# A transformer layer on one core: projections in two pieces, semaphores by part, later coefficient loads, an inverse root on GpSimd, and the third hidden tile first

## The reference

```
x = layernorm(x + attn(x))        # x: 4 batches x 512 tokens x 512
x = layernorm(x + ffn(x))
attn: q,k,v = x @ Wq.T, x @ Wk.T, x @ Wv.T   # 32 query heads of 16, 8 key/value heads (4 queries share one)
      q,k = rope(q), rope(k)
      out = softmax(causal(q k.T / 4)) v ;  out @ Wo.T
ffn:  W = mean_w + mean(|w - mean_w|) * sign(w - mean_w)     # for w1, w2, w3 (512 x 1792)
      silu(x @ W1.T) * (x @ W3.T) @ W2.T
layernorm: (x - mean) / sqrt(var + 1e-5)
```

## Time and profile before

| | us |
|---|---|
| median of 3 runs (lowest, highest) | 992.41 (990.38, 994.47) |
| profiled execution, device time | 995.51 |
| its span from first to last instruction | 993.7 |
| PE busy, PEld busy | 897.1, 609.5 |
| DVE busy | 719.9 |
| ACT busy | 354.0 |
| POOL busy | 258.2 |

### The profile page before, as it was taken

How to read it: one execution, slowest core, us unless ns; L and a number is a source line. 1 busy time by engine, 2 the same in 40 slices (tenths; PEclk the granted TensorE clock), 3 DMA queues, 4 the chain that set the end, 5 groups by cost and what they waited for, 6 DMA issues and landing times.

```text
span 993.7 us, 15538 instructions
## 1 busy us (share of the span) xinstructions
PE 897.1 (90%) x5186; PEld 609.5 (61%) x5186; DVE 719.9 (72%) x1896; ACT 354.0 (36%) x681; POOL 258.2 (26%) x323
## 2 busy tenths in 40 slices
PE   3278998899998999899897999999999999999993
PEld 2144444355443545444476888888888888888882
DVE  7587775776776777766558778777877787778777
ACT  0126665655765556654932111111111111111133
POOL 2046444654357342411333010111011101110000
PEclk9579999999999999999998999999999999999997
DMA  5747776745567623420341011011101110110004
GB/s 174 93 152 175 217 193 209 175 152 137 124 183 189 149 73 82 104 67 23 131 161 63 1 64 42 23 63 63 60 3 63 63 63 0 63 63 0 1 12 159
DMA packets 49692, 95.28 MB, mean 96 GB/s; under 512 B 11424, under 2 KB 25760, under 8 KB 48608
## 3 DMA queue, kind: packets, MB, share of 16 engines
q1 hardware_dynamic: 49632, 94.53, 34.1%
HBM read 66.72 MB, written 14.02 MB: 81 GB/s over the span
## 4 chain that ended last, share of the span: by engine, by line
PE 73%; DVE 11%; DMA 6%; issue 4%; SPq 3%; ACT 2%; POOL 1%; ACTq 0%; DVEq 0%; POOLq 0%
PE PS L970 19%; PE PS L971 18%; PE PS L972 18%; PE PS L1069 5%; PE PS L1096 5%; DVE masked L822 5%; PE PS L1086 4%; DMA Qs<-parts 2%; PE PS L1088 2%; SPq L352 1%; DMA xraw<-xt 1%; DMA o_dram<-Oe 1%; DVE rp L814 1%; ACT Pt L612 1%; DMA Qs<-wo 1%
## 5 line engine op out<-in xcount | busy, mean ns | idle before, releaser
L822 DVE CUSTOM_DVE_ANT_0 masked<-PS,mkw 128x384 bf16<-128x384 f32 (+3 forms) x512 | 230.3, 485 | 109.8 <-PE PS L1069 107.1
L612 ACT ACTIVATE Pt<-PS 128x512 f32<-128x512 f32 (+1 forms) x352 | 190.6, 562 | 153.7 <-PE PS L1088 132.8
L1069 PE MATMUL PS<-Ks,Qs 96*128 96x384 bf16 (+3 forms) x512 | 134.0, 314 | 46.9 <-DVE negM L822 31.2
L970 PE MATMUL PS<-XH,WH 128*128 128x512 f32 x448 | 174.4, 389 | 0.7 <-DVE XL L777 0.7
L972 PE MATMUL PS<-XH,WL 128*128 128x512 f32 x448 | 174.3, 389 | 0.0
L971 PE MATMUL PS<-XL,WH 128*128 128x512 f32 x448 | 174.3, 389 | 0.0
L565 ACT ACTIVATE sg<-PS 128x512 f32<-128x512 f32 x56 | 33.6, 600 | 371.1 <-PE PS L972 371.1
L1086 PE MATMUL PS<-Qs,Ks 99*128 99x256 bf16 (+3 forms) x512 | 139.8, 306 | 3.8 <-DMA Qs<-mT 1.9
L724 DVE TENSOR_TENSOR y<-PS,y 128x512 f32<-128x512 f32 x224 | 138.9, 681 | 1.1 <-PE PS L972 1.1
L472 POOL TENSOR_TENSOR Wr<-Wr 128x512 f32<-128x512 f32 x42 | 53.8, 1312 | 312.6 <-DMA Wr<-wall 312.6
L1069 PEld LDWEIGHTS PS<-Ks,Qs 96*128 96x128 bf16 x512 | 41.4, 99 | 149.5 <-DVE negM L822 100.7
(11 more groups left out here) (101 smaller groups left out, 1233.6 us busy)
## 6 DMA issues: line engine op xcount, KB each, us to landing
co<-wall SPq DMA_DIRECT2D x42, 512.0 KB, 5.7
Wr<-wall SPq DMA_DIRECT2D x42, 512.0 KB, 4.8
Qs<-parts SPq DMA_DIRECT2D x96, 128.0 KB, 3.9
o_dram<-Oe SPq DMA_DIRECT2D x32, 256.0 KB, 3.4
xraw<-xt SPq DMA_DIRECT2D x16, 256.0 KB, 4.0
Oc<-o_dram SPq DMA_DIRECT2D x16, 256.0 KB
y<-x SPq DMA_DIRECT2D x4, 1024.0 KB, 8.2
Inv<-inv_dram SPq DMA_DIRECT2D x16, 256.0 KB
```

The source lines that it names most:

```text
L612: act.activation(Pt[:, t % 2, h:h + m, P * t:S], PS[:, BANKS_P2[(g[0] * NU + n) % 3], 0:m * w].rearrange("p (m w) -> p m w", m=m), ACT.Exp ...
L822: least = dve.tensor_tensor_reduce(masked[:, (g[0] * NU + n) % 2, i * w:(i + 1) * w], bank, mkw[:, S - w:S], -1.0, -MASKED, ALU.add, ALU.m ...
L970: pe.matmul(dst, stH, moH, start=(k == 0), stop=False)
L1069: last = pe.matmul(bank[:, i * w:(i + 1) * w], Qs[0:ROWS, GH * g[1] + h0 + i, P * t:P * (t + 1)], Ks[0:ROWS, g[1], 0:w], start=True, stop= ...
```

## The change

- `project` runs in two pieces of six products, at units 4 and 7, instead of four pieces of three at 3, 5, 7 and 8. `project_out` runs in two pieces of six, at units 8 and 10 (in step 7: 1 and 3), instead of 3, 3 and 6. The two first-pass banks are the same before and after.
- `q_in` and `k_kept` count by part (high, middle, low) instead of by tile. So `high` waits only for the high parts of the tile before, `middle` for the middle ones, and `low` (POOL) for the low one. PE waits for the same transfers as before, through three semaphores.
- The two loads `co` leave the head of SP's list for a step. The first stands behind the maxima `mT` and ahead of the stacking, the second behind the stacking. `diff` and `abs_sum` come one step later, and the first `abs_sum` at unit 5 instead of 8.
- POOL computes the inverse root as a power of -0.5; DVE's reciprocal and ACT's Sqrt go.
- In `first_pair`, DVE makes the third hidden tile (`silu(2, 0)`) ahead of the first `accumulate`, and the third weight tile after the second `accumulate`.

```diff
-PROJECT_AT = (3, 5, 7, 8)
+PROJECT_AT = (4, 7)
...
+BEFORE = {1: (1, 0), 2: (2, 0), 4: (3, 0), 5: (0, 1), 6: (K_TILE, 1)}
...
-        q_in = [sem(f"q_in{i}") for i in range(4)]
-        k_kept = sem("k_kept")
+        q_in = [sem(f"q_in{p}") for p in range(3)]
+        k_kept = [sem(f"k_kept{p}") for p in range(3)]
...
+            def stacked(eng, b, tile, part):
+                eng.wait_ge(q_in[part], 16 * Q_PARTS.count(part) * (QT * b + tile + 1))
+
+            def sent(eng, ps, b, part):
+                tile, late = BEFORE[ps]
+                if tile == K_TILE:
+                    eng.wait_ge(k_kept[part], 16 * (b + late))
+                else:
+                    stacked(eng, b + late, tile, part)
...
-                                             parts[:, part, :]).then_inc(q_in[i], 16)
+                                             parts[:, part, :]).then_inc(q_in[part], 16)
...
-                            if sec.nxt and st < NCO // 2:
-                                load_co(b, 2 * st)
-                                load_co(b, 2 * st + 1)
...
                                 sp.dma_start(Qs[ROWS:ROWS + 3, h:h + GH, :], mT[:]).then_inc(max_in, 16)
+                            if sec.nxt and st < NCO // 2:
+                                load_co(b, 2 * st)
...
                                 stacks(tile, b + (who == "nxt"), r + b * N_ROPE, 2)
+                            if sec.nxt and st < NCO // 2:
+                                load_co(b, 2 * st + 1)
...
-                            if sec.nxt and st < NCO // 2:
-                                diff(b, 2 * st)
+                            if sec.nxt and 0 < st <= NCO // 2:
+                                diff(b, 2 * st - 2)
...
+                                sent(pool, ps, b, 2)
                                 low(r)
-                            if sec.nxt and st < NCO // 2:
-                                diff(b, 2 * st + 1)
+                            if sec.nxt and 0 < st <= NCO // 2:
+                                diff(b, 2 * st - 1)
...
+                            pool.wait_ge(var_out, b)
+                            pool.tensor_tensor(rs[:], sd[:], expo[:], ALU.pow).then_inc(std_out, 1)
                             pool.wait_ge(std_out, b)
                             pool.tensor_tensor(shift[:], mean[:], rs[:], ALU.mult).then_inc(shift_out, 1)
...
-                        act.wait_ge(var2_out, b + 1)
-                        act.activation(rs[:], sd[:], ACT.Sqrt).then_inc(std2_out, 1)
                         act.wait_ge(shift2_out, b + 1)
...
-                                    before = {1: (1, b + 1), 2: (2, b + 1), 4: (3, b + 1), 5: (0, b + 2),
-                                              6: (K_TILE, b + 2)}[ps]
-                                    if before[0] == K_TILE:
-                                        act.wait_ge(k_kept, before[1] * 48 - 48)
-                                    else:
-                                        act.wait_ge(q_in[before[0]], before[1] * 96)
+                                    sent(act, ps, b, 0)
                                     high(r)
                                 if n == 4 and sec.behind(st, 3):
                                     o_copy(sec.behind(st, 3))
                                 if n == 7 and mine:
+                                    sent(act, ps, b, 1)
                                     middle(r)
-                                if n in (8, 10) and sec.nxt and st < NCO // 2:
-                                    abs_sum(b, 2 * st + (n == 10))
-                                if n == 7 and st == 7 and sec.prev:
-                                    act.wait_ge(var_out, b)
-                                    act.activation(rs[:], sd[:], ACT.Sqrt).then_inc(std_out, 1)
+                                if n in (5, 10) and sec.nxt and 0 < st <= NCO // 2:
+                                    abs_sum(b, 2 * st - 2 + (n == 10))
...
                         if n == 2:
-                            act.wait_ge(q_in[0], 96)
+                            stacked(act, 0, 0, 0)
                         high(r)
+                        if n == 2:
+                            stacked(act, 0, 0, 1)
                         middle(r)
                     sections(Run(act, section))
...
-                        a = flink(dve.tensor_scalar(sd[:], mv[:, :, 1], EPS, None, ALU.add))
-                        dve.wait_ge(fchain, a)
-                        dve.reciprocal(sd[:], sd[:]).then_inc(var2_out, 1)
+                        dve.tensor_scalar(sd[:], mv[:, :, 1], EPS, None, ALU.add).then_inc(var2_out, 1)
...
+                            if first and u == 0:
+                                dve.wait_ge(y_done, QT)
+                                silu(2, 0)
                             if first and u == 2:
                                 for m in range((B - 1) * KT + 2, B * KT):
                                     turned_low(m)
-                            if not (last and u == UNITS - 1) and not (first and u == 0):
+                            if not (last and u == UNITS - 1) and not (first and u < 2):
...
                             if first and u == 0:
-                                weights(3, 1, 2)
+                                pass
                             elif b < 3 and not (last and i == 1) and not (first and i == 0):
                                 weights(it * 6 + 3 * i + 3, (i + 1) % 2, b)
                             accumulate(n, FIRST_PAIR[u] % B if first else b)
+                            if first and u == 1:
+                                weights(3, 1, 2)
                             if last and i == 1:
...
                         dve.wait_ge(mid_out, r + 1)
+                        if n == 2:
+                            stacked(dve, 0, 0, 2)
                         dve.tensor_tensor(parts[:, 2], rp[:, 1], parts[:, 1], ALU.subtract).then_inc(lo_out, 1)
...
-                                    pe.wait_ge(q_in[st // 2], (b + 1) * 96)
+                                    for p in range(3):
+                                        stacked(pe, b, st // 2, p)
...
-                                    project(b + (who == "nxt"), tile, up, PROJECT_AT.index(n))
+                                    for k in range(2 * PROJECT_AT.index(n), 2 * PROJECT_AT.index(n) + 2):
+                                        project(b + (who == "nxt"), tile, up, k)
...
-                                    for k in ({1: (0,), 2: (1,), 3: (2, 3)} if st == 7 else {7: (0,), 9: (1,), 10: (2, 3)}
+                                    for k in ({1: (0, 1), 3: (2, 3)} if st == 7 else {8: (0, 1), 10: (2, 3)}
                                               ).get(n, ()):
```

More of the change, by code:

```diff
@@ L236, in layer @@
         asum = top.enter_context(nc.sbuf_tensor("asum", [P, 3, NCO], F32))
-        few = top.enter_context(nc.sbuf_tensor("few", [P, 6, QT], F32))
-        csum, coef, sd, mean, shift, rs = (few[:, n] for n in range(6))
+        few = top.enter_context(nc.sbuf_tensor("few", [P, 7, QT], F32))
+        csum, coef, sd, mean, shift, rs, expo = (few[:, n] for n in range(7))
         onesf = top.enter_context(nc.sbuf_tensor("onesf", [P, P], F32))
@@ L352, in stack_q @@
                                 sp.dma_start(Qs[HD * n:HD * (n + 1), 8 * i:8 * i + 8, :],
-                                             parts[:, part, :]).then_inc(q_in[i], 16)
+                                             parts[:, part, :]).then_inc(q_in[part], 16)
                     def keep_k(r, part, done):
                         hold(sp, done, r + 1, passed)
-                        sp.dma_start(k_dram[part], parts[:, part, :]).then_inc(k_kept, 16)
+                        sp.dma_start(k_dram[part], parts[:, part, :]).then_inc(k_kept[part], 16)
                     def stack_k(b, half):
-                        hold(sp, k_kept, b * 48, passed)
+                        for p in range(3):
+                            sp.wait_ge(k_kept[p], b * 16)
                         h = slice(4 * half, 4 * half + 4)
@@ L552, in _ @@
                     for b in range(B):
+                        pool.wait_ge(var2_out, b + 1)
+                        pool.tensor_tensor(rs[:], sd[:], expo[:], ALU.pow).then_inc(std2_out, 1)
                         pool.wait_ge(std2_out, b + 1)
@@ L853, in statistics @@
                             dve.tensor_scalar(mean[:], mv[:, :, 0], -1.0, None, ALU.mult)
-                            a = link(dve.tensor_scalar(sd[:], mv[:, :, 1], EPS, None, ALU.add))
-                            dve.wait_ge(chain, a)
-                            dve.reciprocal(sd[:], sd[:]).then_inc(var_out, 1)
+                            dve.tensor_scalar(sd[:], mv[:, :, 1], EPS, None, ALU.add).then_inc(var_out, 1)
                     def first_tile(r, n):
@@ L942, in _ @@
                     dve.memset(mp_all[:], 0.0).then_inc(ready0, 1)
+                    dve.memset(expo[:], -0.5)
                     dve.memset(onesf[:], 1.0).then_inc(ready0, 1)
```

2 lines of the change are left out of this document (1 added, 1 removed).

## The result

The changed kernel takes 1002.5 us (median of 6 runs, 998.18 to 1004.92), the kernel before 993.38 in the same session: a ratio of 1.009, 95% interval 1.0059 to 1.0122. I had forecast 984, between 974 and 991, so the sign was wrong too. The profiled execution has a span of 1001.5 us, 7.8 more than before.

A forecast was written before the change was run, and what follows sets the result against it. PE was taken as the bound, with gains only in its attention waits and at feed-forward's ends. Terms -2.0 - 1.0 - 4.0 + 5.1 - 1.2 - 5.0 = -8.1 took the median from 992.4 to 984 us, range 974 to 991.

The forecast's parts named there:

- First tiles: Start of the kernel: three of four operations before DVE's first maximum leave the path; -2.0 us (-1 to -2).
- Six products in a piece: Projections in attention: saved product beginnings gain 5 us, some ten steps starved by DVE lose 4; -1 (-5 to +6).
- Coefficient loads: Attention: section 1, step 1 waits go, -4 (0 to -5); input transfer later in third steps, +5.1 (-4 to +10).
- The inverse root: Section ends: table loads go, 3 x -0.6; DVE waits for POOL's power, 2 x 0.3; -1.2 us (-2 to +2).
- a power over 1 us: Sign at section ends: the forecast counts as wrong if POOL's power takes over 1 us; 0.20 was assumed.
- Feed-forward's start: First units of feed-forward: third hidden tile made earlier, next `gate_up` starts 5.0 us earlier; -5.0 (-3.5 to -6).
- D: Rival: SP's queue becomes the bound, loads waiting for `abs_sum` in twelve steps; slower than before, up to 999; chance 0.08.
- A: Rival: the input transfer is no later, or DVE has slack there; +5.1 becomes about -1, 978; chance 0.27.
- B: Rival: six-product pieces starve DVE in every step with a projection; +6 in place of -1, 991; chance 0.09.
- C: Rival: the power is slow, 1.28 us, at section ends and the kernel's end; about +4, 988; chance 0.10.

The follow-up runs named there:

- c_parts: a_cobefore, but `high` again waits for all six stacking transfers of the tile before; 986.04 us, ratio 0.995 to the kernel before.
- a_cobefore: The changed kernel with only the coefficient loads, subtraction and sum put back as in the kernel before; 979.84 us, ratio 0.9873 to the kernel before.
- c_pow: a_cobefore with ACT's root and DVE's reciprocal again in place of POOL's power; 981.48 us, ratio 0.9909 to the kernel before.
- b_ffn: The kernel before with only feed-forward's beginning changed (third hidden tile first, third weight tile behind the second sum); 985.93 us, ratio 0.9929.
- c_proj: a_cobefore with projections in pieces of three again and the output projection in 3, 3, 6; 985.55 us, ratio 0.9934 to the kernel before.
- a_shift: The changed kernel with both coefficient loads at the head of steps 1 to 7, subtraction and sum in the same step; 986.61 us, ratio 0.9945.
- a_coend: The changed kernel with a step's first coefficient load moved behind the stacking, beside the second; 993.37 us, ratio 1.0017 to the kernel before.
- a_early: The changed kernel with a step's first chunk subtracted at the head of POOL's step and summed at unit 1, not 5; 999.56 us, ratio 1.0092.

## Why the prediction was wrong, point by point

**First tiles: right.** PE's first wait for the maxima, at its second batch of products, is 2.0 shorter than the 2.58 of before, and undone in c_parts it comes back (2.65):

```profile
43.68 0.39 PE L1084 MATMUL PS<-Ks,Qs 96*128 96x256 bf16 x1 [0.60 <-DVE negM L836]
```

**Six products in a piece: -1 predicted, 0 alone and about -6 among the others.** Both halves of the term are in the steps: 1.5 and 1.6, with three beginnings saved in each, take 15.43 instead of 15.79 (0.12 for each, where I had 0.08), and step 1.2 takes 13.01 instead of 12.66, the loss of 0.4 that I had expected. What I left out is that the pieces also decide how far PE is when the input transfer comes. That the median of the whole then moved by 6 among the others was not in my term.

**Coefficient loads: the failed step.** Two terms, -4 for the waits that go and +5.1 for the later input transfer, made +1.1; measured is +22.7 (the changed kernel against a_cobefore). By steps, in one execution of each: input transfer (0.4, 1.3 + 1.4, 2.3 + 2.4) +6.0, +4.9, +5.7, together 16.6; border of sections 0 and 1 (0.7, 1.0, 1.1) +2.8, +4.8, -5.0, together +2.6 against my -4; the rest, 0.7 to 0.9 each in 0.1 to 0.3, 2.0 and 3.0, against 0. My +5.1 had counted in what the semaphores by part give back, so for it the kernel before is the fair measure: there the three places grew by 6.4, 3.6 and 3.9, together 13.9, where I had 3.4, 1.2 and 1.0, together 5.6. So that term came out 2.5 times as large, and of the -4 nothing was left, since 0.7 and 1.0 lost more than 1.1 gained. The mechanism of the +5.1 was right and its first link exact. Three sizes were missing:
- Bytes. I counted a load ahead of the transfer as 0.6 us of issue. It is 512 KB that are still under way when `xraw` is issued: in section 0 the load is issued at 90.87 and lands at 95.4, `xraw` is issued at 93.20. In a_cobefore both loads had landed by then, 2.9 us before `xraw`. The DMA share doesn't tell the two apart (1.02 and 1.09 above, 1.04 and 1.12 in a_cobefore from 88 to 96 us). The landing became 1 us longer in section 0, and 1.5 to 2.4 longer in sections 1 and 2. I had asked how long SP stands, and not what the engines carry.
- The clock. Behind a PE wait of 4.2 us stand 6.8 us at 0.50; in a_cobefore the clock stays at 1.00 there. Step 0.4 is 6.0 longer than in a_cobefore, while PE's idle time in it is 3.3 longer (4.67 against 1.37). The other 2.7 I put down to the clock: 6.8 us at half speed lose 3.4 at most. In a sum of idle times it doesn't appear.
- Absorption. For sections 1 and 2 I let the new delay swallow the waits that stood there. That did happen to PE's wait for Oe (1.73 to 0.36 in section 1), but the delay was larger than what it swallowed: PE then stood 2.92 us for the maxima in section 1, step 4 (at most 0.5 before), and 1.54 and 3.41 in section 2 (1.36 before).

And in the -4 I asked what takes the place of the wait for POOL only with the loads of `y` in mind, as a bound of 0 and without a price. What took its place is SP's own queue, in steps 0.7 and 1.0.

**The inverse root: -1.2 predicted, -1.6 by the medians (c_pow), which can't be told from 0, with the price wrong.** I had taken 0.20 for the power from the multiplication of the same shape, with 1.28 as the upper bound. It is 1.02, and the row behind it is that multiplication:

```profile
272.70 1.02 POOL L558 TENSOR_TENSOR few<-few 128x4 f32<-128x4 f32 x1
273.80 0.20 POOL L560 TENSOR_TENSOR few<-few 128x4 f32<-128x4 f32 x1
```

DVE stands 0.70 for it at a section's end. Against that stand the table loads of ACT, and the last stretch, from section 3, step 7 on, which is 0.9 shorter with the power (525.0 against 525.9 in c_pow). The sum had a slip too: I wrote that DVE stands 0.4, and counted 0.3. My own condition "a power over 1 us" was met and didn't decide.

**Feed-forward's start: right.** -5.0 predicted, -5.0 in b_ffn's profile, -6.0 by its medians. In the changed kernel's trace:

```profile
548.77 0.33 PE L1034 MATMUL PS<-idf,y 128*128 128x128 f32 x1 [0.53 <-DVE hL L728]
...
557.80 0.50 PE L985 MATMUL PS<-XH,WH 128*128 128x512 f32 x1 [1.52 <-DVE XL L791]
```

The transposes start at 548.77, which is 535.0 without the 13.8 us that attention is longer, as forecast. The idle time before them is 0.53 (5.23 before); a new one of 1.52 stands two units later. DVE's cast took 0.84 at 547.16, while POOL subtracted until 547.7; the same cast takes 0.43 at 559.11, with POOL idle. The Trainium skill (SBUF — State Buffer, the part on the shared port pair) has the loser of that port pair block until the other instruction ends, and by that the cast would end some 0.4 after 547.7. It ended at 548.0, so the trace agrees to 0.1.

**The rivals.** D had the right engine and the right sign, at 0.08, but spread the delay over twelve steps, where it stands in three places and at the border. I had looked for its damage at `den`, and dismissed it since `den` has slack; the input transfer and the maxima, in the same queue, have none. A and B fell (`xraw` was not issued earlier, the pieces did not cost), C fell as well: the power took 1.02, and c_pow shows no loss by it. Without the two terms of the loads my sum is -9.2, and a_cobefore measured 12 to 13. That these are near each other is in part luck: the pieces gave 6 and not 1, `high` by part more than the 2.0 of the first tiles, and undone one by one (c_proj 5.7, c_parts 6.2, c_pow 1.6, b_ffn 6.0) the parts come to 19.5, so they overlap. The part that failed cost more than all the others gained.

## What to carry to other kernels

An edit that moves a load within an in-order DMA queue moves everything behind it, so price it for each transfer behind it, by when that one is needed and not by what the queue waits on average, and price it twice: the wait at the head, and the bytes that are under way when the urgent transfer is issued. A prefetch that no one waits for did best here at the head of a step, behind `Inv`, where its bytes landed before the urgent transfer was issued. POOL's 64 us of waiting less bought 5 us in one step and lost them in the two before it, since PE waits at three or four places only; ask of each such place what would be late next, and count the stretch at half clock that can stand behind a long PE wait.

## What the runs showed of the hardware

- A power of 128x4 on GpSimd took 1.02 us, five times a multiplication of the same shape (0.20).
- A transfer of 256 KB took 3.6 to 4.6 us from issue to landing when the 512 KB loads ahead of it had landed, or did so within 0.2 us (a_cobefore and a_shift, step 3 of sections 0 to 2), 4.9 to 6.2 with one of them under way (the changed kernel), and up to 10.7 with two (a_coend and a_early, section 2), though the share of the DMA engines was 1.0 to 1.1 in a_cobefore too. One of 12 KB took 8.4 behind a 512 KB and a 1 MB load.
- The granted clock does not follow the length of a single wait. In the changed kernel it fell to 0.50 behind 4.20 us of idle PE (99 us), in a_coend it stayed at 1.00 behind 2.78 us (146 us) and fell to 0.50 for the stretch 204 to 208 behind one of only 2.1 us (202 us).
